# One GpSimd queue of gathers, paced by TensorE: a wait behind every second gather for first and second products in turn, in place of one behind every third for first products

## What is computed

```
x = x + gnn0(norm(x), adj)      # adj@x, W1, rmsnorm, silu, W2
x = x + moe0(norm(x), edges)    # graph attention over 524288 edges gives scores; best 2 of 4 experts
x = x + gat1(norm(x), adj)      # masked softmax over adj, elu
x = x + moe1(norm(x))           # softmax gate; best 2 of 8 experts, H = 256

# attention over edges in moe0, 4 heads x 4 channels
e     = leaky_relu(a_src[src] + a_dst[dst])
alpha = exp(e) / segment_sum(exp(e), dst)
agg   = segment_sum(h[src] * alpha, dst)
# each expert
y = gelu(x @ W1[e] + b1[e]) @ W2[e] + b2[e]
```

## Time and profile before

| what | value |
|---|---|
| median of 3 runs | 3724.08 us (3717.02 to 3727.64) |
| the profiled execution, its own time | 3701.19 us |
| its span in the profile | 3699.5 us |
| TensorE clock granted, mean | 0.83 of full |
| busy: TensorE, VectorE, ScalarE, GpSimd | 2668, 2761, 1719, 1160 us |

### The profile page before, as it was taken

The page is one execution under the profiler, slowest core; times in us unless marked ns, Lnnn a source line. Parts: engine busy times, 40 slices in busy tenths (PEclk is TensorE's granted clock), DMA queues, the critical chain, the costliest instruction groups (busy, mean ns, idle before and its releaser), DMA issues.

```text
span 3699.5 us, 49643 instructions
## 1 busy us (share of the span) xinstructions
PE 2668.0 (72%) x15405; PEld 1958.2 (53%) x15406; DVE 2760.9 (75%) x8056; ACT 1718.6 (46%) x3052; POOL 1160.4 (31%) x1205
## 2 busy tenths in 40 slices
PE   1788888888888612027877777778787777787789
PEld 1566656665666401025555555555555555555566
DVE  7788778877788546367877787787787787777774
ACT  1556556665666311124444454444544544444544
POOL 0000000000000037665555545545545555455100
PEclk9899999999999855557877878878878778887889
DMA  2111111111110123223223222232232322322200
GB/s 83 40 39 49 41 46 52 41 46 35 44 44 35 72 61 77 45 65 76 60 62 79 61 70 68 57 77 61 59 76 64 78 63 58 77 60 60 73 12 9
DMA packets 228561, 210.53 MB, mean 57 GB/s; under 512 B 70781, under 2 KB 160585, under 8 KB 227657
## 3 DMA queue, kind: packets, MB, share of 16 engines
q1 hardware_dynamic: 190008, 190.83, 17.3%
q0 software_dynamic: 37280, 14.38, 4.3%
q10 hardware_dynamic: 1008, 2.15, 0.2%
HBM read 159.49 MB, written 47.74 MB: 56 GB/s over the span
## 4 chain that ended last, share of the span: by engine, by line
PE 21%; DVE 20%; issue 10%; another core or an unknown queue 8%; ACT 3%; POOL 2%; DVEq 0%; DMA 0%; SPq 0%; ACTq 0%; POOLq 0%
PE lay_b_z L1780 9%; PE lay_b_y L1789 8%; DVE keep_x L2163 5%; POOL lay_got L1743 2%; ACT lay_unused L2012 1%; DVE lay_oh L1047 1%; ACT lay_hid L1934 1%; DVE lay_oht L2068 1%; PE lay_b_att L1757 1%; PE lay_b_b L1829 1%; DVE lay_left L1059 1%; DVE lay_parts L1060 1%; DVE lay_parts L1058 1%; DVE lay_parts L1061 1%
## 5 line engine op out<-in xcount | busy, mean ns | idle before, releaser
L1743 POOL DMA_INDIRECT lay_got<-node_table,lay_idx x1152 | 1137.2, 987 | 952.1 <-PE lay_b_z L1780 381.0
L1789 PEld LDWEIGHTS lay_b_y<-lay_w,lay_hid 128*128 128x128 f32 x4096 | 586.7, 219 | 294.5 <-issue 283.6
L1789 PE MATMUL lay_b_y<-lay_w,lay_hid 128*128 128x128 f32 x4096 | 593.6, 302 | 106.8 <-issue 79.7
L1780 PE MATMUL lay_b_z<-lay_xin,lay_w 128*128 128x512 f32 x1024 | 652.1, 771 | 19.2 <-ACT lay_hid L1934 14.2
L1934 ACT ACTIVATE lay_hid<-lay_b_z,lay_b 128x512 f32<-128x512 f32 x512 | 330.1, 683 | 464.1 <-PE lay_b_z L1780 275.8
L2163 DVE SCALAR_TENSOR_TENSOR keep_x<-lay_b_y,lay_gates,keep_x 128x128 f32<-128x128 f32 x1024 | 287.8, 343 | 319.6 <-issue 130.1
L871 POOL MEMSET find_no_src<- 128x9 int32 x1 | 0.1, 107 | 1261.7 <-POOLq L47 1261.7
L2012 ACT ACTIVATE lay_unused<-lay_hub_wide,lay_halves 128x1152 bf16<-128x1152 uint16 x256 | 320.3, 1251 | 115.5 <-DMA lay_hub_wide<-sorted_dst 111.1
L1780 PEld LDWEIGHTS lay_b_z<-lay_xin,lay_w 128*128 128x128 f32 x1024 | 221.7, 240 | 206.6 <-issue 174.8
L460 PE MATMUL front_b_h<-front_xt,front_m 128*128 128x512 f32 x512 | 271.7, 664 | 56.6 <-DVE front_hb L701 34.1
L217 DVE TENSOR_TENSOR sort_keys<-sort_keys 128x1024 f32<-128x1024 f32 (+2 forms) x182 | 257.4, 1414 | 31.8 <-ACT sort_keys L538 29.3
(11 more groups left out here) (392 smaller groups left out, 4518.2 us busy)
## 6 DMA issues: line engine op xcount, KB each, us to landing
lay_wide<-sorted_dst SPq DMA_DIRECT2D x128, 288.0 KB
lay_hub_wide<-sorted_dst SPq DMA_DIRECT2D x128, 288.0 KB
made<-front_y SPq DMA_DIRECT2D x128, 256.0 KB, 2.0
lay_y<-made SPq DMA_DIRECT2D x32, 1024.0 KB
lay_got<-node_table,lay_idx POOLq DMA_INDIRECT x1152
front_adj<-in_adj SPq DMA_DIRECT2D x32, 256.0 KB, 3.1
keep_x<-in_x SPq DMA_DIRECT2D x32, 256.0 KB, 3.4
lay_adj<-in_adj SPq DMA_DIRECT2D x32, 256.0 KB
```

The source lines that it names most:

```text
L1743: pool.indirect_dma_start(out=got[:, b % RING, c, :], out_offset=None, in_=table, in_offset=bass.IndirectOffsetOnAxis(ap=idx[:, b % AHEAD, ...
L1780: pe.matmul(b_z[c][:, :], w1[:, e, P * c:P * c + P], flat(xin[g % 2][:, :, :]), start=True, stop=True).then_inc(z_done, 1)
L1789: mm = pe.matmul(b_y[n % 2][:, P * j:P * j + P], hid[n % 2][:, c, P * j:P * j + P], w2[:, e * HK + c, :], start=(c == 0), stop=(c == HK - 1))
```

## The change

Behind the edit GpSimd waits ahead of gather 2 and 6 for z_done, and ahead of gather 4 and 8 for y_done, where it waited ahead of 3 and 6 for z_done. Nothing else differs.

```diff
                 n = E1 * ((b - RING - 2) // 4 - QUAD - 2) + 2 * ((b - RING - 2) % 4)
                 for c in range(GC):
-                    if c % 3 == 0 and c > 0:
-                        after(pool, z_done, HK * min(n + 1 + c // 3, groups * E1) if n >= 0 else 0)
+
+                    if c % 4 == 2:
+                        after(pool, z_done, HK * min(n + 2 + c // 4, groups * E1) if n >= 0 else 0)
+                    elif c % 4 == 0 and c > 0:
+                        after(pool, y_done, min(n + c // 4, groups * E1) if n >= 0 else 0)
                     pool.indirect_dma_start(
```

## The result

The changed kernel takes 3688.5 us (nine runs, 3677.0 to 3705.8) against 3724.1: a ratio of 0.991 (0.9893 to 0.9928, a 95% interval), 35 us less. A second set on another chip gives 0.9929 (0.9906 to 0.9952; 3667.5 against 3693.0 us). The direction was as forecast, the size less than half of the 80 us.

A forecast was written before the change was run, and what follows sets the result against it. No engine was full; the prediction took TensorE's completions to be held by strings of GpSimd gathers. 26.5 groups at 3.0 us gave 80 us, so 3724 - 80 = 3644 us, range 3585 to 3762.

The forecast's parts named there:

- the 80 us: Whole gain forecast for the paced last stage: 26.5 groups of four blocks at 3.0 us each.
- the mechanism: TensorE's completions are held while GpSimd's gathers follow each other, from about the fifth, and let go when the string ends.
- The rival that the grouping doesn't matter: Late signals have another author than the gather strings; time stays at 3724 us, within 11; chance 0.16.
- the slow rival: Each string, however short, holds completions to its end, so more stops are slower: 3760 to 3796 us; chance 0.22.
- the replay: Walk through one group's dense stretch with the new waits: strings of 5 and 6, gain 1.25 to 6.25 us.
- The sketch of what the profile after would show: Strings at most 5 or 6, smaller remote waits at L1934, L1971 and L1983, group period about 64 us.
- the term of 3.0 us a group: Cutting a group's three long gather strings (9, 6, 9) wins 1.0 us each.
- the replay's low end of 1.25: Gain per group if only the first string's earlier release counts: 1.25 us, 33 us over 26.5 groups.
- all four waits count alike: Waits at gathers 2, 4, 6 and 8 were valued together, by string length: 3 x 1.0 us a group.
- the ceiling of 17 us a group: The 36 gathers of a group cost it some 17 us, the most any placing of gathers can win.
- an added wait that is met costs GpSimd nothing: The 212 added waits in 106 blocks were bounded by 0 and 0.3 us each and taken as 0.
- the remote waits of L1983 and L1971 fell: Waits on late signals at these readers in the last stage should fall well below 176 and 161 us.

The follow-up runs named there:

- one_gather: Kernel before the change with only gather 0 of each block, the other eight left out: ratio 0.9115, 3398.9 us.
- fill: Kernel before the change with eight of nine gathers replaced by GpSimd fills of an unused tile, about 1 us each: ratio 0.9522, 3551.7 us.
- sync_dma: Kernel before the change with each block's nine gathers replaced by direct transfers of neighbouring rows, issued by SyncE: ratio 0.9146, 3410.0 us.
- pause3: Kernel before the change plus a 128 x 1024 float fill that GpSimd waits for, ahead of gathers 0, 3 and 6 of each paced block: ratio 0.9687.
- pause3_short: Kernel before the change plus a 256-column fill that GpSimd waits for, ahead of gathers 0, 3 and 6: ratio 0.9939.
- pause_two: Kernel before the change plus a 1024-column fill that GpSimd waits for, ahead of gathers 0 and 5 alone: ratio 0.9749.
- no_y4: Changed kernel without its wait ahead of gather 4, so waits at 2 and 6 for first products and 8 for a second: ratio 0.9832 to before.
- no_y8: Changed kernel without its wait ahead of gather 8, so waits at 2 and 6 for first products and 4 for a second: ratio 1.0098 to before.
- seq_pause: Kernel before the change plus twenty GpSimd waits on a counter long since met, ahead of gathers 0, 3 and 6, no fill: ratio 1.0056.
- z4: Changed kernel's four wait places (2, 4, 6, 8), but all waiting on first products, whole or half: ratio 1.0058 to before.
- land3: Kernel before the change, with GpSimd waiting ahead of gathers 0, 3 and 6 until all issued gathers have landed, no fill: ratio 1.0422.

## Why the prediction was wrong in size

**Right: the mechanism.** Signals of TensorE are held while gathers follow each other and let go when they stop; one_gather, fill, sync_dma and pause3 show it. One thing it lacked: a stop has to last, since 0.60 us behind each third gather let little go (pause3_short). The rival that the grouping doesn't matter is out, and the slow rival (each string costs its own hold) too: pause3 has 12 strings a group in place of 7 and is the faster.

**Wrong: the replay, by which "one met wait gives 2, and 3 across the edge" cuts the long strings to 5 and 6.** The sketch of what the profile after would show asked for strings of at most 5 or 6; they were 7, 7, 6 and 7, and up to 11. The replay let two waits be met in its first string and three in its second, and only its first crossed a block's edge. In the profile after each of the strings shown passes three, the one that opens it counted: at 2396.59 first product 10,5 (ended 2392.34) and second product 10,4 (2394.13) were both out, and first product 10,6 ended at 2399.04, within the string's third gather, and was still seen; where a block's edge lies inside, that makes 7 gathers. The mean string fell from 6.2 to 5.9. With 24 of a group's gathers in strings of 5 and 6 and the other 12 in strings of 2 and 3 it would have been some 4.5, an estimate; at 4.1 (pause_two) a group gains 3.6 us. So it was the cut that was too small, as far as these two can be compared, since pause_two makes its stops by other means.

**Mis-sized: the term of 3.0 us a group.** It took 1.0 us from joining three strings late in the group and used it three times, though the groups with equal strings that gave it spread over 1.8 us by themselves (66.7 to 68.5), and of two more of their kind, left out of the mean, one takes 64.7 us (from 2815.5), with its last nine gathers as 6 and 3. Measured, the change is worth 35.5 / 26.5 = 1.3 us a group. That is near the replay's low end of 1.25, which I had kept as a bound. Nor does the mean string set the price by itself: with the wait at 8 beside those at 2 and 6, no_y4 wins 1.7% with strings that are no shorter than before's (6.6). That it hangs on which signals a string covers is likely and not shown.

**Wrong: all four waits count alike.** The forecast summed over strings; the waits at 2, 6 and 4 together lose 1% (no_y8), and the one at 8 wins it back and more.

**Wrong, without effect on the sum: the ceiling of 17 us a group.** It is 7.6 for 32 of the 36 gathers (one_gather).

**Right:** an added wait that is met costs GpSimd nothing (twenty in seq_pause leave the 0.30 us between gathers), no more gathers came late for VectorE (over the whole trace it waited 18.7 us for them in 5 cases, 21.4 in 7 before), and the remote waits of L1983 and L1971 fell. The forecast that L1934's would fall too failed: 181.7 to 207.3 us.

**Open:** why the wait at 4 costs. With it the gelu's longest remote wait is 8.7 us, without it (no_y4) 5.8, and VectorE's sum is late by 166 and 139 us; but the reader of L1971 goes the other way, 29.0 us with it and 162.3 without. That the stop at 4 moves the next string over gelu's signals is a guess from this. How GpSimd's gathers hold the signals is not shown by a profile either. TensorE's granted clock over the 25 groups is higher in every kernel that wins (0.80 before; 0.82 changed, 0.83 in pause3, 0.86 in one_gather), and no run tells how much of a gain is the clock's. no_y4 with a pause was not tried.

## What to carry to other kernels

When signals of one engine come late, all at once, and just behind the end of another engine's series, test the series by itself: leave it out, replace it by idle work, issue it from elsewhere. A wait paces only while it is unmet; where the pacer runs late, only a pause that it cannot skip cuts a string for sure, and a deliberate stop of 0.9 us on an engine with room won 3.4% here, almost four times the finer waits. Try several lengths of it: 0.60 us won 0.6%. What a wait waits for counts, and not the number of waits: four at the same four gathers won 0.9% (the change) or lost 0.6% (z4). To put the wait on the signal that the late reader needs, since the stop is what frees it, is worth a try; the runs here don't prove it. And count a reader's idle time under all its names before saying that a hold moved.

## What the hardware showed that I had not expected

Indirect DMAs of 128 rows, issued by GpSimd one per 1.25 us, held TensorE's completions for up to 8.6 us in the string of nine shown; 3 in a row with 1.25 us between strings hardly did (pause3), with 0.60 us between them they did (pause3_short), and nine direct DMAs a block from SyncE didn't. Twenty waits that were already met fitted into the 0.30 us between two gathers. A fill of 128 x 1024 floats on GpSimd took 0.97 us and cost VectorE 0.22 us on the average (2.7 us for 12 in pause3), 0.15 us in fill (4.8 us for 32). Behind a run of three gathers GpSimd stood 2.5 us on the average until it saw them landed, while other transfers ran (land3).
